# Decoder layer on one core: an own staging buffer for the FFN weight pieces, later queue waits, cross products placed ahead of skipped chunks, last outputs around the last unit

## The reference, cut to what matters

```python
x = layernorm(x + attn(x))       # 32 query heads in 8 groups: grouped KV attention @ w_o
                                 # plus latent attention (lk, lv from x @ w_lq, x @ w_lv) @ w_lo, causal
x = layernorm(x + fake_quant(x) @ fake_quant(ctx_4096))          # per batch, 0..255, rounded
x_scale = 448 / max(abs(x)); w_scale = 448 / max(abs(weight))    # over the whole tensors
x = layernorm(x + clip(x * x_scale) @ clip(weight * w_scale) / (x_scale * w_scale))
```

## Time and profile before

| | us |
|---|---|
| median of 3 executions | 2635.64 (2631.15 to 2638.55) |
| the profiled execution, its own time | 2634.64 |
| span of the profiled execution | 2632.7 |
| TensorE matmuls busy | 2498.0, 95% of the span |
| VectorE busy | 1720.8, 65% |
| ScalarE busy | 1133.9, 43% |
| GpSimd busy | 917.1, 35% |

### The profile page before, as it was taken

The page is one execution under the profiler, slowest core; times in us unless marked ns, Lnnn a source line. Parts: engine busy times, 40 slices in busy tenths (PEclk is TensorE's granted clock), DMA queues, the critical chain, the costliest instruction groups (busy, mean ns, idle before and its releaser), DMA issues.

```text
span 2632.7 us, 40708 instructions
## 1 busy us (share of the span) xinstructions
PE 2498.0 (95%) x12452; PEld 2109.7 (80%) x12456; DVE 1720.8 (65%) x3589; ACT 1133.9 (43%) x2576; POOL 917.1 (35%) x696
## 2 busy tenths in 40 slices
PE   8799999999999999999888989899898989989898
PEld 6688888888888888887667878788787878878777
DVE  5676767677676767665856666566566556657565
ACT  3444435353444444443643444434344443434451
POOL 4333342424243343424514333242433424233210
PEclk9999999999999999999999999999999999999999
DMA  5223232323232232324223223231322323124411
GB/s 174 88 69 93 73 96 60 100 60 92 60 99 69 71 90 68 91 69 127 88 100 114 67 72 92 68 104 48 103 61 84 92 68 100 56 86 125 168 33 64
DMA packets 124407, 226.26 MB, mean 86 GB/s; under 512 B 13088, under 2 KB 21408, under 8 KB 124192
## 3 DMA queue, kind: packets, MB, share of 16 engines
q1 hardware_dynamic: 119552, 216.91, 27.5%
q10 hardware_dynamic: 4768, 8.39, 0.9%
HBM read 206.37 MB, written 18.87 MB: 86 GB/s over the span
## 4 chain that ended last, share of the span: by engine, by line
PE 52%; issue 30%; POOL 13%; DVE 2%; ACT 1%; DMA 1%; POOLq 0%; SPq 0%; DVEq 0%; PEldq 0%; ACTq 0%
POOL w_lo L405 12%; PE bank_a L1185 9%; PE bank_a L1186 9%; PE bank_a L1187 9%; PE bank_b L1185 7%; PE bank_b L1186 7%; PE bank_b L1187 7%; PE bank_b L1233 3%; PE bank_b L1493 1%; DMA w_raw<-wstream 1%; ACT probs L506 0%; DMA probs<-xt 0%; DVE probs L800 0%; DVE pT_lo L817 0%; ACT w_hi L469 0%
## 5 line engine op out<-in xcount | busy, mean ns | idle before, releaser
L405 POOL TENSOR_TENSOR w_lo<-w_raw,w_hi 128x512 fp32r<-128x512 f32 x632 | 840.1, 1337 | 1380.0 <-ACT w_hi L469 1362.9
L469 ACT ACTIVATE w_hi<-w_raw 128x512 fp32r<-128x512 f32 x632 | 393.6, 626 | 420.6 <-DMA w_raw<-wstream 250.5
L1185 PE MATMUL bank_a<-w_hi,o_hi 128*128 128x512 f32 x1024 | 413.3, 404 | 10.1 <-DVE acc L881 5.4
L817 DVE TENSOR_TENSOR pT_lo<-bank_b,pT_hi 128x512 fp32r<-128x512 f32 (+1 forms) x384 | 207.5, 595 | 315.5 <-ACT pT_hi L512 315.3
L1187 PE MATMUL bank_a<-w_hi,o_lo 128*128 128x512 f32 x1024 | 404.9, 395 | 0.0
L1186 PE MATMUL bank_a<-w_lo,o_hi 128*128 128x512 f32 x1024 | 404.8, 395 | 0.0
L506 ACT ACTIVATE probs<-probs,row_min 128x512 f32<-128x512 f32 (+3 forms) x512 | 281.5, 551 | 247.9 <-DVE row_min L800 245.6
L516 ACT ACTIVATE o_hi<-bank_b 128x512 fp32r<-128x512 f32 x128 | 76.6, 599 | 430.9 <-PE bank_b L1187 430.9
L811 DVE TENSOR_SCALAR probs<-probs,row_inv 128x512 f32<-128x512 f32 (+3 forms) x512 | 254.4, 557 | 4.5
L1185 PEld LDWEIGHTS bank_a<-w_hi,o_hi 128*128 128x128 f32 x1024 | 195.0, 190 | 45.5 <-issue 7.7
L1187 PEld LDWEIGHTS bank_a<-w_hi,o_lo 128*128 128x128 f32 x1024 | 194.3, 190 | 42.5
(11 more groups left out here) (176 smaller groups left out, 4838.5 us busy)
## 6 DMA issues: line engine op xcount, KB each, us to landing
w_raw<-wstream SPq DMA_DIRECT2D x632, 256.0 KB, 2.7
stage<-ctx SPq DMA_DIRECT2D x32, 256.0 KB, 2.8
stage<-wf SPq DMA_DIRECT2D x32, 256.0 KB, 2.7
q_scratch<-stage_q SPq DMA_DIRECT2D x32, 128.0 KB, 1.7
wf_hi_scratch<-piece_hi SPq DMA_DIRECT2D x16, 256.0 KB, 2.1
wf_lo_scratch<-stage SPq DMA_DIRECT2D x16, 256.0 KB, 2.3
wf_hi<-wf_hi_scratch SPq DMA_DIRECT2D x8, 512.0 KB, 7.6
wf_lo<-wf_lo_scratch SPq DMA_DIRECT2D x8, 512.0 KB, 11.2
```

The lines of the kernel that those rows point to most:

```text
L405: nc.gpsimd.tensor_tensor(w_lo[:, s], w_raw[:, r], w_hi[:, s].bitcast(F32), ALU.subtract).then_inc(lo_done, 1)
L469: nc.scalar.activation(w_hi[:, s], w_raw[:, r], ACT.Copy).then_inc(hi_done, 1)
L817: nc.vector.tensor_tensor(pT_lo[:, at:at + w], BANK_B[bank][:, 0:w], pT_hi[:, at:at + w].bitcast(F32), ALU.subtract).then_inc(pT_lo_done, 1)
L1185: nc.tensor.matmul(dst, still[0], move[0], start=start, stop=False)
```

## The change

The FFN weight pieces get a buffer `stage_w` and a semaphore `wf_in`; `stage` is left to the context. SP loads them at chunks 4 and 25 and stores the splits at 0 (of the next group) and 22; the q2 stores stand at 14 and 30. VectorE treats the first piece right after the first context piece, the second after unit 1. ScalarE's `piece_high` stands at chunks 12 and 29, GpSimd's `piece_low` at 17 and 33. No piece of work is added.

In the first group of batch 1 a slot does its cross product before its chunks, the cross products stand in slots 1 to 4, the skipped chunks are spread up to slot 5 and the first own output is in slot 5 in place of 7. VectorE does the residual of each half at the start of units 0 and 1 and its statistics at their end (before: middle of units 0 and 2). ScalarE stores and reloads the halves at chunks 26, 28, 28, 30.

At the end of a batch the outputs 0 and 1 stand ahead of the last `values`, and only output 3 waits for the last `o_lo`. The first two FFN transposes follow output 3 as before. The scratch for dynamic DMA goes from 1024 to 512.

```diff
@@ -46,8 +46,8 @@
...
-NEXT_PARTS = [(0, 1), (2, 3), (4, 5), (6,), (7,), (), (), (8,), (9,), (), (10,), (11,), (12,), (13,), (14,), (15,)]
-CROSS_PARTS = {1: (0, 0), 2: (0, 1), 4: (1, 0), 5: (1, 1)}
+NEXT_PARTS = [(0,), (1,), (2, 3), (4,), (5, 6), (7, 8), (), (9,), (), (10,), (), (11,), (12,), (13,), (14,), (15,)]
+CROSS_PARTS = {1: (0, 0), 2: (0, 1), 3: (1, 0), 4: (1, 1)}
@@ -127,7 +127,7 @@
...
         col_part = sb("col_part", [P, 2, N], F32)
-        piece_hi = sb("piece_hi", [P, N], F32R)
+        stage_w, piece_hi = sb("stage_w", [P, N], F32), sb("piece_hi", [P, N], F32R)
@@ -236,6 +236,7 @@
...
         piece_turn = sem("piece_turn")
+        wf_in = sem("wf_in")
@@ -299,37 +300,45 @@
...
                 sp.dma_start(wf_hi_dram[m], piece_hi[:].bitcast(F32)).then_inc(wf_out, 16)
-                sp.dma_start(wf_lo_dram[m], stage[:]).then_inc(wf_out, 16)
+                sp.dma_start(wf_lo_dram[m], stage_w[:]).then_inc(wf_out, 16)
+            def load_wf(b, g, j):
+                G = g + KVH * b
+                if b == 0:
+                    wait(sp, w_part_done, 2 * G + j)
+                elif j or not isinstance(g, int) or g:
+                    sp.wait_ge(wf_out, 64 * g + 32 * j)
+                else:
+                    sp.wait_ge(w_part_done, 2 * KVH)
+                sp.sem_inc(piece_turn, 1)
+                sp.dma_start(stage_w[:], wf[2 * g + j]).then_inc(wf_in, 16)
...
                 G = g + KVH * b
+                if c == 0 and b and not (isinstance(g, int) and g == 0):
+                    store_split(2 * g - 1)
...
-                    if b == 0:
-                        wait(sp, w_part_done, 2 * G)
-                    elif isinstance(g, int) and g == 0:
-                        sp.wait_ge(w_part_done, 2 * KVH)
-                    else:
-                        store_split(2 * g - 1)
-                        sp.wait_ge(wf_out, 64 * g)
+                    wait(sp, q2_done, 2 * G)
...
                     sp.dma_start(stage[:], ctxt[2 * G]).then_inc(stage_in, 16)
-                if c in (14, 26):
-                    j = (14, 26).index(c)
+                if c == 4:
+                    load_wf(b, g, 0)
+                if c in (14, 30):
+                    j = (14, 30).index(c)
...
                     sp.dma_start(q2_dram[2 * G + j], stage_q[:]).then_inc(q2_out, 16)
-                    sp.dma_start(stage[:], wf[2 * g] if j else ctxt[2 * G + 1]).then_inc(stage_in, 16)
-                if c == 34:
-                    if b == 0:
-                        sp.wait_ge(w_part_done, 2 * G + 1)
-                    else:
-                        store_split(2 * g)
-                        sp.wait_ge(wf_out, 64 * g + 32)
-                    sp.sem_inc(piece_turn, 1)
-                    sp.dma_start(stage[:], wf[2 * g + 1]).then_inc(stage_in, 16)
+                    if j == 0:
+                        sp.dma_start(stage[:], ctxt[2 * G + 1]).then_inc(stage_in, 16)
+                if c == 22 and b:
+                    store_split(2 * g)
+                if c == 25:
+                    load_wf(b, g, 1)
@@ -414,7 +423,7 @@
...
                 pool.wait_ge(piece_hi_done, m + 1)
-                nc.gpsimd.tensor_tensor(stage[:].bitcast(F32R), stage[:], piece_hi[:].bitcast(F32),
+                nc.gpsimd.tensor_tensor(stage_w[:].bitcast(F32R), stage_w[:], piece_hi[:].bitcast(F32),
@@ -434,8 +443,8 @@
...
                         add_corr(c - C_PREV, corr0)
-                    if b and c in (33, 37):
-                        piece_low(2 * g + (33, 37).index(c))
+                    if b and c in (17, 33):
+                        piece_low(2 * g + (17, 33).index(c))
@@ -525,7 +534,7 @@
...
-                act.wait_ge(stage_in, 16 * (4 * G + j + 1))
+                act.wait_ge(stage_in, 16 * (2 * G + j + 1))
@@ -534,7 +543,7 @@
...
                 wait(act, wf_out, 32 * m)
-                nc.scalar.activation(piece_hi[:], stage[:], ACT.Copy).then_inc(piece_hi_done, 1)
+                nc.scalar.activation(piece_hi[:], stage_w[:], ACT.Copy).then_inc(piece_hi_done, 1)
@@ -614,10 +623,10 @@
...
                         copy_q1T(t)
-                if c in (27, 31):
-                    store_r((27, 31).index(c))
-                if c in (29, 33):
-                    load_acc((29, 33).index(c))
+                if c in (28, 30):
+                    load_acc((28, 30).index(c))
+                if c in (26, 28):
+                    store_r((26, 28).index(c))
@@ -663,8 +672,8 @@
...
                             crossed(c)
-                        if b and c in (29, 35):
-                            piece_high(2 * g + (29, 35).index(c))
+                    if b and c in (12, 29):
+                        piece_high(2 * g + (12, 29).index(c))
@@ -850,10 +859,10 @@
...
                 m = 2 * G + j
-                dve.wait_ge(stage_in, 16 * (4 * G + 3 + j))
+                dve.wait_ge(wf_in, 16 * (m + 1))
                 wait(dve, w_run_done, m)
-                nc.vector.tensor_reduce(col(W_PART), stage[:], mybir.AxisListType.X, ALU.max,
+                nc.vector.tensor_reduce(col(W_PART), stage_w[:], mybir.AxisListType.X, ALU.max,
@@ -861,10 +870,10 @@
...
                 m = 2 * g + j
-                dve.wait_ge(stage_in, 16 * (4 * (g + KVH) + 3 + j))
-                nc.vector.tensor_scalar(stage[:], stage[:], col(WS), FP8_MAX, ALU.mult, ALU.min).then_inc(w_scaled, 1)
+                dve.wait_ge(wf_in, 16 * (2 * KVH + m + 1))
+                nc.vector.tensor_scalar(stage_w[:], stage_w[:], col(WS), FP8_MAX, ALU.mult, ALU.min).then_inc(w_scaled, 1)
                 dve.wait_ge(w_scaled, m + 1)
-                nc.vector.tensor_scalar(stage[:], stage[:], -FP8_MAX, None, ALU.max).then_inc(w_clipped, 1)
+                nc.vector.tensor_scalar(stage_w[:], stage_w[:], -FP8_MAX, None, ALU.max).then_inc(w_clipped, 1)
@@ -907,6 +916,13 @@
...
+            def weight_piece(b, g, j):
+                if b == 0:
+                    largest_weight(g, j)
+                else:
+                    clip_weights(g, j)
@@ -928,6 +944,7 @@
...
                         quantise_piece(b, G, 0)
+                        weight_piece(b, g, 0)
@@ -948,14 +965,12 @@
...
                 for u in range(UNITS):
+                    if u < 2 and first and b:
+                        for t in range(TT):
+                            cross_residual(t, u)
...
                         normalise(G, u + 1)
-                    if u in (0, 2) and first and b:
-                        for t in range(TT):
-                            cross_residual(t, u // 2)
-                        for t in range(TT):
-                            half_stats_of_r(t, u // 2)
@@ -964,11 +979,11 @@
...
                         mask_scores(G, u + 2)
-                    if u in (1, 4):
-                        if b == 0:
-                            largest_weight(G, (1, 4).index(u))
-                        else:
-                            clip_weights(g, (1, 4).index(u))
+                    if u < 2 and first and b:
+                        for t in range(TT):
+                            half_stats_of_r(t, u)
+                    if u == 1:
+                        weight_piece(b, g, 1)
@@ -1407,14 +1422,14 @@
...
                 def part(slot):
-                    for i in ((NEXT_PARTS if b else FIRST_PARTS)[slot] if first else (slot,)):
-                        prev(i) if i < 8 else own(i - 8)
...
                         early_cross(*CROSS_PARTS[slot])
+                    for i in ((NEXT_PARTS if b else FIRST_PARTS)[slot] if first else (slot,)):
+                        prev(i) if i < 8 else own(i - 8)
@@ -1431,6 +1446,11 @@
...
+            def last_output(b, i):
+                p = 4 * KVH * (b + 1) - 2
+                output(b, KVH, i, TAIL_POS + i, i, p, 4, lambda t: (added, 4 * (p - 1) + t + 1))
@@ -1459,12 +1479,16 @@
...
                     group(b, g, False)
-                values(KVH * (b + 1) - 1, UNITS - 1)
-                p = 4 * KVH * (b + 1) - 2
-                pe.wait_ge(o_lo_done, UNITS * KVH * (b + 1))
+                for i in range(C_TAIL // 2):
+                    if i == 2:
+                        values(KVH * (b + 1) - 1, UNITS - 1)
+                    if i in (0, 3):
+                        pe.wait_ge(o_lo_done, UNITS * KVH * (b + 1) - (0 if i else 1))
+                    last_output(b, i)
                 if b + 1 < B:
-                    for i in range(C_TAIL):
-                        output(b, KVH, i, TAIL_POS + i, i, p, 4, lambda t: (added, 4 * (p - 1) + t + 1))
+                    for i in range(C_TAIL // 2, C_TAIL):
+                        last_output(b, i)
@@ -1515,12 +1539,11 @@
...
             b = B - 1
-            for i in range(C_TAIL):
-                output(b, KVH, i, TAIL_POS + i, i, p, 4, lambda t: (added, 4 * (p - 1) + t + 1))
-                if i == 3:
-                    pe.wait_ge(pT_lo_done, 3 * UNITS * KVH * B)
-                    transpose_x2(0)
```

(8 more changed lines are left out.)

## The result

The changed kernel takes 2532.19 us (median of 4 runs, 2531.13 to 2533.28) against 2633.88 (4 runs, 2631.15 to 2638.55) before: a ratio of 0.9607, 95% interval 0.9594 to 0.9621. The forecast was 2536 with a range of 2522 to 2562. The profiled execution took 2531.58 with a span of 2529.6, so the spans differ by 2632.7 - 2529.6 = 103.1, where the sum of the forecast was 99.6.

A forecast was written before the change was run, and what follows sets the result against it. Batch 0's groups were bound by TensorE's matmuls, batch 1's also by SP's chunk loads and ScalarE waiting on each other. 73.0 + 2.2 + 19 - 2 + 7.4 = 99.6 off 2634.64 gives 2535.0, median 2536, range 2522 to 2562.

The forecast's parts named there:

- groups 9 to 14: Batch 1's steady groups: would run at batch 0's pace, saving 73.0 us; bounds nothing or all of it.
- group 8: First group of batch 1, 173.83 us: gains at transposes, middle and end sum to 21.4; given 19, from 12 to 24.
- between the batches: Batch 1's first product waits for GpSimd although outputs 0 and 1 fill TensorE: 2 us lost, bounds -4 and +4.
- end of the attention: Seventh `values` of group 15 to the FFN: 38.26 us falls to 30.9; gain 7.4, bounds 4 and 9.8.
- The ring: Batch 1: SP's chunk loads wait for an FFN piece whose producer ScalarE waits for those loads; 12.17 us a group.
- Rival 1: A wait remains in batch 1's groups, half of the 73.0 is left: 2572 to 2573 us; chance 0.16.
- Rival 2: Moved clips: VectorE and GpSimd hold each other up, 2.1 us in each of 8 groups: 2553 us; chance 0.08.
- Rival 3: Stall belongs to the late exponentials of the last units, not the pieces: 2630, up to 2636 us; chance 0.03.
- rival 4: Slower: VectorE waits for `wf_in` ahead of q rotations, TensorE loses 7.18 in all 16 groups: 2651 us; chance 0.03.
- The 2.4 taken off for a slow clock: Group 8: idle time before and after `scores` may lower the clock; 2.4 us deducted from the 21.4 gain.
- the ring's share of this group: Group 8, from `values` of unit 2 to the end: 7 to 9 us of the 15.1 gain.
- TensorE waits about 9 us in place of 2.17: Before batch 1's first product: TensorE waits for GpSimd, then starts at 1.2 GHz; a loss of 2 us.

The follow-up runs named there:

- buffer_only: Kernel before with only a separate buffer for the weight pieces; every load, wait, clip, split and store in its old place: 2636.7 us, ratio 1.0005.
- waits_later: Kernel before, shared buffer kept; only SP's two blocking places moved three chunks back (1 to 4, 34 to 37): 2554.53 us, ratio 0.9688.
- no_last: Changed kernel with the last outputs again behind the last `values` in both batches: 2534.97 us, ratio 0.9607.
- pieces_only: Kernel before with the weight pieces' own buffer and all their new places; group 8's order and last outputs as before: 2541.64 us, ratio 0.9649.
- The three parts alone: Three kernels, each the kernel before with one part: the pieces, group 8's new order, or the last outputs moved; ratios 0.9649, 0.9985, 0.9999.
- early_reduce: Changed kernel with GpSimd's reduction of the weight maximum behind the fourth tail chunk instead of the eighth: 2527.19 us, ratio 0.9586.
- add_first: Changed kernel with VectorE's first `add_part` of the tail output ahead of the two `x_low`: 2534.69 us, ratio 0.9616.
- both: Changed kernel with the edits of early_reduce and add_first together: 2525.0 us, ratio 0.9577.
- both_front: both, plus in batch 1's first group `corr0` adds two chunks earlier and second context piece behind the first masks: 2520.19 us, ratio 0.9553.

## Why the prediction was right, point by point

| term of the sum | forecast | measured | from |
|---|---|---|---|
| groups 9 to 14 | -73.0 | -72.9 | 935.29, 862.35 |
| group 15 to its seventh `values` | -2.2 | -2.2 | 145.03, 142.85 |
| group 8 | -19 (12 to 24) | -20.3 | 173.83, 153.53 |
| between the batches | +2 (-4 to +4) | +1.0 | 192.31, 193.27 |
| end of the attention | -7.4 | -7.7 | 38.26, 30.59 |
| start, up to group 1 | 0 | -0.9 | 167.9, 167.0 |
| sum | -99.6 | -103.1 | spans |

- **Steady groups.** The ring was read rightly and is shown: `buffer_only` leaves it, `waits_later` breaks it with the shared buffer. The prediction named the place of SP's waits, not the buffer, and that is what decides. Rival 1 (a remaining wait) fell: six groups at batch 0's pace. Beside 42.9 us in six waits for `pT_lo`, groups 9 to 14 had lost 11.1 in six waits for masked scores and some 19 by the slow clock (881.33 busy for 862.28); all of it went. Rival 2 fell in this kernel (clips of 0.48 and 0.43, 7.34 of cover behind them), though `waits_later` has a wait of its kind, 1.51 a group. Rival 3 fell by the windows, rival 4 by the clips that start without a wait.
- **Group 8.** By its own marks: the first `transposes` began 0.4 earlier (1305.35), forecast 1.2; from there to `values` of unit 2 (1333.22) 5.3, forecast 5.1; from there to the end 42.86 in place of 57.41, 14.55, forecast 15.1. The 2.4 taken off for a slow clock was not paid: up to the first transposes TensorE was busy for 75.89 at a clock of 0.96 before as well as after, and behind them the clock was 1.00. The mis-sized part is the ring's share of this group: I wrote 7 to 9, and the pieces alone bring 12.6, the order 7.7 and not the 12 to 14 that were left to it of 21.4. So 20.3 for 19 is partly luck: the ring's share was too low, the order's too high, and the deduction was not needed.
- **Between the batches.** The start of the first product was forecast at 1208.5 and measured at 1208.55, with luck, since group 7 began 0.9 earlier; from there it took 179.3 in place of 178.3. "TensorE waits about 9 us in place of 2.17" is right as a sum of waits and wrong as one wait for GpSimd. The waits are 1.00, 4.80 and 3.04: the step left out VectorE, behind whose `x_low` the emptying of `bank_a` stands. The slow restart was paid, but behind the 4.80, ahead of the first product: the first 4.76 us there ran at 0.51. The clock was 1.00 again behind the 3.04. The kernel before had a longer slow stretch, from 1176.71 to 1187.00 at 0.50 to 0.55, which the forecast didn't count. From group 7's start to group 8's the idle time rose by 2.7 (7.53 to 10.26) and the busy time fell by 1.8 (184.78 to 183.01), in sum the 1.0.
- **End.** The size was right (7.7), and so were the terms: 28.95 of work for 28.5, waits of 1.0 and 0.5 for 1.2 and 1.2. Its source was right only in part: the forecast gave all of it to the last outputs. The pieces' new places alone bring 4.3 (`no_last`, 33.97) to 5.6 (`pieces_only`, 32.63), the outputs the other 2.0 to 3.4. Of the three waits of this end before (1.52 for `normalise`, 3.14 for `pT_lo`, 1.41 for `o_lo`) the pieces' places take away the first and 0.6 of the second, and part of the slow clock (0.87 to 0.95 and 1.00). `waits_later`, without the ring but with the late split, keeps all three.
- **Parts and whole.** The three parts alone give, by ratio, 3.51% + 0.15% + 0.01% = 3.67%; together they give 3.93%. The difference is some 7 us, of which 4.4 is the order's gain in group 8 that the ring took away (7.7 against 3.3).
- **The forecast's own range.** Its terms, best and worst, add up to 2522.6 and 2554.4, not to 2524 and 2552. The measured time lies in both.

The GpSimd idle times around its reduction were 6.87 and 6.75, after 7.24 and 7.27 before the change. The Trainium skill (GPSIMD Engine Reference, 2.1 "Instruction dispatch") has 5.95 us for the first call of freshly loaded code. The rows here, 6.38 to 6.87 ahead of the reduction in the changed kernel and `early_reduce`, lie above it, and the measured ones decide; that the time is spent on loading code no run here shows.

## What to carry to other kernels

In an engine's or a DMA queue's fixed order, a wait belongs a few steps behind its producer and behind every load that the producer itself needs; if it stands ahead of them the ring closes at each turn, and a separate buffer alone did not help here (ratio 1.0005). Find such a loss by comparing windows of groups with equal work, then follow the waits until an engine comes up twice. And where two engines hold back the same place one behind the other, removing the earlier one alone gains nothing and removing the later one only its own part (3.4); the rest comes when both go (8.3).

## What was not expected of the hardware

The same stretch of work, from the first product of batch 1 to group 8, took 14.0 us in the changed kernel and 16.27 in `add_first`, by the granted clock alone:
```profile
1208.55:1222.55 14.00, 12.59 (x52) 9.63 (x53) 1.93 (x6) 4.76 (x8) 10.32 (x9) 1.00 0.60 188
```
```profile
1208.18:1224.45 16.27, 14.86 (x51) 11.30 (x52) 1.87 (x6) 4.76 (x8) 10.25 (x9) 0.85 0.53 162
```
TensorE had stood idle for 3.04 ahead of the first and for 10.96 ahead of the second. `both` had the slow form too (15.6, clock 0.89) behind a wait of only 2.02, and `no_last` (15.65, clock 0.89) behind 2.83, while `both_front` had the fast one (13.98, clock 1.00) behind 1.76. So the length of the wait just ahead does not tell which it will be. That is 1.6 to 2.3 us by which an edit of a few microseconds can look better or worse than it is.

The window also hides a part. The changed kernel had its slow stretch earlier, right behind the wait of 4.80:
```profile
1192.15:1196.91 4.76, 4.76 (x11) 3.76 (x12) 4.76 (x8) 1.24 (x2) 0.38 (x1) 0.51 0.59 202
```
From group 7's start to group 8's TensorE was busy for 183.01 in the changed kernel and for 182.82 in `add_first`. Over the whole stretch the two paid alike for the clock, and what `add_first` loses (196.20 against 193.27) is idle time. A stretch has to be long enough to hold every slow restart before its clock is compared.
